# Gathered attention: identity products before its first sixteen transposes, and scatters and gathers spread over the steps

## What is computed

```python
# layer 6: one shared expert for all tokens, and one of 7 experts for each token
x = x + L2_ffn(layernorm(x))      # 0.5/total * shared(x) + p * expert[argmax](x) / total
# layer 7: attention of x over the context, 128 sequences of 64 tokens, one head of 128
logits = q @ k.T / sqrt(128); logits = where(mask == 0, NEG, logits)
o = layernorm(softmax(logits) @ v) * gamma + beta
x = x + o
```

## Time and profile before

| what | value |
|---|---|
| median of three runs | 2151.9 us |
| the profiled execution | 2150.0 us, of which the span on the core is 2148.3 us |
| mean granted TensorE clock over the span | 0.923 |
| swiglu, from its first transpose to its last store | about 1337 to 1632 us of the span |
| gather_attention, from its first gather to its last statistics | about 1636 to 1824 us of the span |
| busy over the span: PE, DVE, ACT, POOL | 89%, 76%, 64%, 51% |

### The profile page before, as it was taken

How to read it: one execution, slowest core, us unless ns; L and a number is a source line. 1 busy time by engine, 2 the same in 40 slices (tenths; PEclk the granted TensorE clock), 3 DMA queues, 4 the chain that set the end, 5 groups by cost and what they waited for, 6 DMA issues and landing times. The chain is left out here.

```text
span 2148.3 us, 86799 instructions
## 1 busy us (share of the span) xinstructions
PE 1907.1 (89%) x32111; PEld 1451.7 (68%) x32111; DVE 1628.0 (76%) x3712; ACT 1364.7 (64%) x3729; POOL 1104.0 (51%) x1286
## 2 busy tenths in 40 slices
PE   5999987989999979999989995999993973799998
PEld 3777754767777758888867773887772431677776
DVE  6788877866777768888856667777664786699998
ACT  4677766655555545666645554667772753599997
POOL 5566632873333325555568882756775754233332
PEclk9999996999999989999999997999996555799999
DMA  5111111000000002000001110113442520000000
GB/s 123 46 47 48 48 40 39 21 6 18 14 14 15 14 27 87 1 0 0 0 21 35 35 30 16 47 61 110 139 142 76 145 70 22 2 17 15 15 15 21
DMA packets 174358, 87.98 MB, mean 41 GB/s; under 512 B 70892, under 2 KB 168840, under 8 KB 174216
## 3 DMA queue, kind: packets, MB, share of 16 engines
q1 hardware_dynamic: 163656, 63.36, 11.0%
q0 software_dynamic: 7296, 21.38, 3.4%
q10 hardware_dynamic: 3264, 1.38, 0.3%
HBM read 66.13 MB, written 19.93 MB: 40 GB/s over the span
## 5 line engine op out<-in xcount | busy, mean ns | idle before, releaser
L1494 POOL TENSOR_TENSOR L1f_hl<-L1f_h,L1f_hh 128x512 fp32r<-128x512 f32 x128 | 167.2, 1307 | 126.1 <-DVE L1f_hh L1506 125.8
L1455 ACT ACTIVATE L1f_h<-L1f_H,L1f_w_b 128x512 f32<-128x512 f32 x192 | 132.0, 688 | 104.9 <-PE L1f_H L925 98.0
L399 POOL TENSOR_TENSOR L1a_wide<-L1a_flat,head_of_row 128x512 f32<-128x512 f32 x64 | 66.6, 1040 | 200.6 <-ACT L1a_flat L597 158.3
L399 POOL TENSOR_TENSOR L3f_wide<-L3f_flat,head_of_row 128x512 f32<-128x512 f32 x64 | 66.7, 1042 | 189.9 <-PE L3f_S L469 167.6
L1506 DVE CAST L1f_hh<-L1f_h 128x512 fp32r<-128x512 f32 x192 | 127.8, 672 | 31.7 <-ACT L1f_h L1455 30.6
L625 DVE TENSOR_REDUCE L1a_mx<-L1a_S 128x16 f32<-128x1024 f32 x64 | 78.4, 1224 | 80.8 <-PE L1a_S L469 80.8
L1841 ACT ACTIVATE L2f_both_act<-L2f_both_A 128x512 f32<-128x512 f32 x114 | 68.2, 598 | 92.1 <-PE L2f_both_G L925 91.2
L1872 DVE TENSOR_TENSOR L2f_both_h<-L2f_both_G,L2f_both_act 128x512 f32<-128x512 f32 x114 | 78.2, 686 | 63.6 <-ACT L2f_both_act L1841 63.1
L399 POOL TENSOR_TENSOR L0a_wide<-L0a_flat,head_of_row 128x512 f32<-128x512 f32 x64 | 66.6, 1040 | 95.0 <-ACT L0a_xhat L610 90.1
L625 DVE TENSOR_REDUCE L0a_mx<-L0a_S 128x16 f32<-128x1024 f32 x64 | 78.3, 1224 | 31.1 <-PE L0a_S L469 31.0
L1778 POOL TENSOR_TENSOR L2f_both_hl<-L2f_both_h,L2f_both_hh 128x512 fp32r<-128x512 f32 x66 | 85.6, 1297 | 31.4 <-ACT L2f_both_hh L1846 26.6
(11 more groups left out here) (534 smaller groups left out, 6815.6 us busy)
## 6 DMA issues: line engine op xcount, KB each, us to landing
L0a_mask_raw<-mask SPq DMA_DIRECT2D x256, 32.0 KB, 1.8
sorted_x<-L1f_zero SPq DMA_DIRECT2D x4, 1408.0 KB, 12.3
L2f_both_xhat<-sorted_x SPq DMA_DIRECT2D x22, 256.0 KB, 3.9
sorted_y<-L2f_both_y_out SPq DMA_DIRECT2D x22, 256.0 KB, 3.9
L0a_ctxT<-ctx_T SPq DMA_DIRECT2D x64, 64.0 KB, 1.9
L1a_ctxT<-ctx_T SPq DMA_DIRECT2D x64, 64.0 KB
L1a_mask_raw<-mask SPq DMA_DIRECT2D x256, 0.1 KB
L2a_ctxT<-ctx_T SPq DMA_DIRECT2D x64, 64.0 KB
```

Source lines behind the costliest of these rows:

```text
L399: pool.tensor_tensor(wide[:, s], flat[:, s, :].rearrange("p (b n) -> p b n", b=B2).unsqueeze(2).broadcast_to([P, B2, 4, S]), c.head_of_row ...
L1455: act.activation(h[:, q % 3, :], psH[:, q % 2, :], ACT.Relu, bias=b1[:, q:q + 1]).then_inc(h_kept, 1)
L1494: pool.tensor_tensor(hl[:, q % 3, :], h[:, q % 3, :], hh[:, q % 3, :], ALU.subtract).then_inc(hl_pool, 1)
```

## The change

Three edits. In swiglu, 8 scatters stay at the head of POOL's list; the other 56 go into its steps, four for each shared group u = 0 to 13 (two, one and one in the parts q), each behind a wait for the up-products of that part. In gather_attention, gathers of tiles 0 to 19 stay at the head of POOL's list (FREE = 20); the gather of tile t from 20 on stands in step t - 10 (AHEAD = 10), behind a wait for the transposes of tiles 0 to t - 22 (at least for the first). And on PE, ahead of the transpose of tiles 0 to 15, stand unread products of the bf16 identity with itself, 48 at tile 0, behind a wait for the statistics of the first eight tiles, and 8 at each of the others, in all 48 + 15 x 8 = 168. They write a part of the PSUM tile that nothing reads.

```diff
 def swiglu(c, name, sems, r, IP, E):
+    EARLY = 8
...
         @block.gpsimd
         def _(pool):
-            for t in range(NT):
+            def scatter(t):
                 pool.indirect_dma_start(r.sorted_x, bass.IndirectOffsetOnAxis(ap=r.place[:, t:t + 1], axis=0),
                                         r.xhat[:, t, :], None).then_inc(scattered, 16)
 
+            for t in range(EARLY):
+                scatter(t)
+
             def step(i, r_):
                 for q in range(IC):
+                    for u, s in shared_at(i, r_, 2):
+                        first = EARLY + u * GT + (0, 2, 3)[q]
+                        for t in range(first, min(first + (2, 1, 1)[q], NT)):
+                            wait(pool, a_done, u * IC + q + 1)
+                            scatter(t)
...
 def gather_attention(...):
-    LAST, AHEAD = 20, 24
+    LAST, AHEAD, FREE = 20, 10, 20
...
             @block.gpsimd
-                for i in range(-AHEAD, NT + 44):
-                    for t, q in at(i, -AHEAD):
+                for i in range(-FREE, NT + 44):
+                    early = range(i + FREE, i + FREE + 1) if i < 0 else ()
+                    late = range(i + AHEAD, i + AHEAD + 1) if FREE <= i + AHEAD < NT else ()
+                    for t in (*early, *late):
                         n = t // GR
                         if t % GR == 0 and n >= 2:
                             pool.wait_ge(gathered[n % 2], 16 * GR * (n // 2))
+                        if t >= FREE:
+                            pool.wait_ge(xT_done, max(t - FREE - 1, 1))
                         pool.indirect_dma_start(r.xhat[:, t, :], None, r.sorted_y, ...
...
             @block.tensor
                     for u, s in at(i, 12):
+                        wait(pe, xT_kept, u - 1)
+                        if u == 0:
+                            pe.wait_ge(x_stats, GR)
+                        for _ in range(48 if u == 0 else 8 if u < 16 else 0):
+                            pe.matmul(psX[:, u % 2, P:2 * P], c.ident_bf[:, :], c.ident_bf[:, :], start=True,
+                                      stop=True, skip_group_check=True)
                         wait(pe, xhat_made, u + 1)
-                        wait(pe, xT_kept, u - 1)
                         pe.transpose(psX[:, u % 2, 0:P], xhat[:, s, :], c.ident[:, :]).then_inc(xT_done, 1)
```

## The result

The kernel after took 2155.78 us (median of 20 runs, 2151.21 to 2159.65), the kernel before 2151.78 beside it (20 runs, 2149.36 to 2156.65). The ratio is 1.0017, 95% interval 1.001 to 1.0024: 2.2 to 5.2 us slower. The forecast was 2143.0 with 2139 to 2155, so the time fell outside the range and on the other side of no change.

A forecast was written before the change was run, and what follows sets the result against it. It took PE to bound swiglu, and in gathered attention PE, then DVE, then an 11.15 us stall behind POOL's 64 gathers. 2150.0 - 9.1 = 2140.9 profiled, plus 1.9 for the median, gave 2143, range 2139 to 2155.

The forecast's parts named there:

- Swiglu's scatters at 0: Spreading swiglu's scatters costs 0: the first load goes 5 to 6 us later, hidden by PE's shared products.
- The stall of 11.15 us goes: Gathered attention: DVE's idle before step 48 vanishes, as L2074 ends at 1716.1 instead of about 1727.
- The 9.1: Gathered attention: net gain in us at DVE's step 56, 1739.1 against 1748.20, already holding 1.0 lost at step 32.
- gather 20's wait: Gathered attention: gather 20 waits for the first transpose, over at 1662.2 against issue at 1661.3 before; this part costs 1.0 us.
- DVE's pace "carried over": Gathered attention: DVE's time for each step is kept, since POOL's tensor operations stay at 48; only what it waits for moves.
- The wait for transpose t - 22, taken as 0: POOL in gathered attention: 5.3 us against 5.1, about even at half clock; 0 to 0.7 us for each of two groups.
- its sign of failing: The prediction fails if the clock is down at first tiles, or DVE waits over a us each for later groups' gathers.
- The products as free: PE in gathered attention: the 48 run in idle time; eight a tile cost nothing at full clock, 1.4 us a step.
- rival A: PE in gathered attention: clock up for most of the first 16 tiles; 2143, range 2140 to 2147, chance 0.48.
- rival B: PE in gathered attention: clock down, products partly hidden, step 32 about 9 to 11 us late; net 0, 2152, chance 0.29.
- Step 32 was to be at 1694 if right: DVE's step 32 in gathered attention: 1694 if right, after 1702 if wrong; it was at 1693.04 before.
- C: Gathered attention: clock down, all products on the path, 15.8 us late at step 32, less 10.1; 2157.6, chance 0.11.

The follow-up runs named there:

- the second kind: Sets of runs in which the kernel before had a median of 2252.6 or 2249.8 us, against 2152 to 2154 in the other sets.
- f3: Kernel before with only the new place of the gathers, without the wait for transposes and without products: stage 175.92 us, ratio 0.9964.
- e1: Kernel before with the 168 identity products alone: stage 182.82 us against 183.00, ratio 0.9997.
- the first kind: Sets of runs in which the median of the kernel before was 2152 to 2154 us, as in the result.

## Why the prediction was wrong

- **Swiglu's scatters at 0:** right. The first load of sorted tokens is issued at 1445.51, PE wants it at 1454.91 and is full. This execution is 2.0 us late there already, so the load compares as 1443.5 with the forecast 1444.1 to 1445.1. SP's queue and PE's transpose in after, beside the earlier trace rows:

```profile
1445.51 0.40 SPq L1747 DMA_DIRECT2D L2f_both_xhat<-sorted_x  x1
```

```profile
1454.91 0.60 PE L1832 MATMUL L2f_both_psT<-ident,L2f_both_xhat 128*128 128x128 f32 x4
```

  I never asked whether the cover holds in every run; 64 us hang on that in the second kind.
- **The stall of 11.15 us goes:** right for the order, which leaves none of it (f3). The 2.76 us left in the kernel after come with the wait. The 9.1 held 1.0 for gather 20's wait, so the order by itself was put at 10.1, and measured 7.1: 3.0 short. The step was DVE's pace "carried over". By it step 32 keeps its place in the order alone; in f3 it comes 2.8 us late though the gathers are there, because two short operations of DVE now meet beta additions of POOL. From there to step 48 f3 takes 27.7 us against a forecast of 27.9, and to step 56 17.6 against 17.2. That the first of these fits is luck: 2.9 us less to step 44 and 2.8 more behind it.
- **The wait for transpose t - 22, taken as 0, bound 0.7 us for each of two groups:** this step failed, and it is the largest. The wait measured 5.7 to 6.1 us, where the prediction had 1.0 for gather 20 (measured 1.0 at step 16) and 0 for the rest: 5.1 short. I compared 5.3 us of latency with 5.1 of lead and called it even for two groups. But a wait that is just late closes a loop (late gather, late group, late transpose, later gather), and it stood ahead of all gathers from 20 on, not of two groups. DVE's waits at the groups are 1.09 us at most in the kernel after, about the size that the prediction named as its sign of failing, so that sign was too coarse: the sum of the small ones and of the stall left over is the loss.
- **The products as free:** the 48 are (0.2). All together they cost 2.4 us of the stage with the wait, 2.9 without it. The clock fell in the gap behind the 48, which the prediction saw as likely. Behind it neither the clock of rival A nor that of rival B came: it was up for about half of the first 16 tiles (0.77 in the mean). And a step of PE there took 31.8 / 16 = 1.99 us, not the 1.4 that the prediction took for a step at full clock.
- **The sum:** forecast -10.1 for the order, +1.0 for the wait, 0 for the products; measured -7.1, +6.1 and +2.4, which is +1.4, and the stage shows +1.46. Step 32 was to be at 1694 if right, after 1702 if wrong. Lined up at the first gather it came at 1699.4, between the two. The rivals B and C had it late because of the products; of its 6.3 us, 2.8 are the order (f3), 0.7 the wait and 2.8 the products, and the deciding loss came behind it. So the time lies between B and C, and not for their reason.
- **The rest of the result:** 1.5 us of the stage would be a ratio of 1.0007, and the interval begins at 1.001. Some 0.7 us or more is not in this stage of the profiled execution. Ahead of the stage profiled executions differ by 4.4 us whatever the kernel; this stays open.

## What to carry to other kernels

Price a wait for pacing by the slack of the whole loop that it closes, and give it steps to spare: four tiles more brought back 4.8 to 6.7 us. Unread products were free where their engine had nothing to do; those in its stream brought the clock up for half of the stretch; by the stage they cost nothing in the old order (e1) and 0.5 to 2.9 us in the new one. When a stall is removed, measure the pace of its neighbours again and do not carry it over. A long run of back-to-back indirect transfers cost nothing in one set and 64 us in another, so its spreading is judged on more than one. Of the kernels here the order with the loose wait and no products was 0.9967 of before in the first kind, and 0.9659 in the second, where the kernel after had 0.9617 to 0.9629.

## What was not expected of the hardware

Beside POOL's back-to-back scatters, two executions of the same code of swiglu had PE busy for 89 of 90 us in one and for 25 in the other, where DVE and ACT stood for up to 24 us at a time, with DMA engines busy at 0.17 and 0.18 of the time. And DVE, with nothing to wait for, needed 26.06 us for what took 21.81 when POOL's tensor operations fell elsewhere.
